# Decoder layer with a masked self-attention, a cross-attention and experts: end of a head, context halves and next loads moved

## What is computed

```python
x = layernorm(x + self_attention(x))            # causal, rope, 32 heads of 16
x = layernorm(x + cross_attention(x, context))  # 32 query heads of 128, 8 key/value heads, 1601 keys
x = layernorm(x + x @ base_W.T + lora(x))       # 28 experts of rank 8, top 2 by a gate
```

## Time and profile before

| | us |
|---|---|
| median of 3 runs | 2866.11 |
| lowest and highest | 2860.11 and 2867.98 |
| the profiled execution | 2861.03 |
| its span, first to last instruction | 2859.2 |

### The profile page before, as it was taken

One profiled execution on the slowest core, in us unless ns is written; L12 is line 12 of the kernel. 1 busy time (PEld: TensorE's weight loads), 2 busy tenths in 40 slices (PEclk: granted clock), 3 DMA queues, 4 the chain that ended last, 5 costly groups with the idle time before them and its releaser, 6 DMA issues. The chain is left out here.

```text
span 2859.2 us, 60441 instructions
## 1 busy us (share of the span) xinstructions
PE 2682.2 (94%) x20528; PEld 2488.0 (87%) x20528; DVE 2081.0 (73%) x4144; ACT 1943.2 (68%) x4158; POOL 1651.6 (58%) x1674
## 2 busy tenths in 40 slices
PE   7889999999889999999988999999988999999997
PEld 5789999898669999999867999999976899999995
DVE  4488787878548878787855878787775587878785
ACT  4476676667547777677664767777766576777674
POOL 3389898957216656565712656665551365656563
PEclk9999999999999999999999999999999999999998
DMA  6356464612411212121331112122142121213111
GB/s 212 129 176 226 166 225 163 210 53 80 174 45 39 97 53 97 48 102 45 119 120 52 67 68 74 67 71 79 55 158 80 51 82 53 97 45 104 45 53 59
DMA packets 89999, 281.69 MB, mean 99 GB/s; under 512 B 9056, under 2 KB 9184, under 8 KB 86624
## 3 DMA queue, kind: packets, MB, share of 16 engines
q1 hardware_dynamic: 89696, 277.82, 28.1%
HBM read 233.75 MB, written 44.04 MB: 97 GB/s over the span
## 5 line engine op out<-in xcount | busy, mean ns | idle before, releaser
L564 POOL TENSOR_TENSOR kept_s<-kept_s,mrow 128x512 f32<-128x512 f32 (+1 forms) x896 | 1065.6, 1220 | 574.1 <-ACT mrow L800 574.1
L1127 DVE TENSOR_TENSOR pl<-sp,ph 128x512 fp32r<-128x512 f32 (+1 forms) x896 | 576.2, 643 | 60.2 <-ACT sp L815 59.2
L810 ACT ACTIVATE ph<-kept_s 128x512 fp32r<-128x512 f32 (+1 forms) x896 | 534.0, 596 | 47.0 <-POOL kept_s L564 41.8
L815 ACT ACTIVATE sp<-kept_s 128x512 f32<-128x512 f32 (+1 forms) x896 | 506.3, 565 | 5.1 <-DVE sua L1135 5.0
L1201 PE MATMUL dn<-ph,vh 128*128 128x256 f32 (+1 forms) x1664 | 490.4, 295 | 2.3 <-DVE pl L1127 1.3
L1201 PE MATMUL dn<-ph,vl 128*128 128x256 f32 (+1 forms) x1664 | 472.9, 284 | 0.0
L1201 PE MATMUL dn<-pl,vh 128*128 128x256 f32 (+1 forms) x1664 | 471.8, 284 | 0.0
L1135 DVE TENSOR_TENSOR sua<-sp,sua 128x512 f32<-128x512 f32 (+1 forms) x640 | 399.6, 624 | 0.0
L792 ACT ACTIVATE kept_s<-bank 128x512 f32<-128x512 f32 x384 | 228.4, 595 | 226.1 <-PE bank L1201 224.5
L792 ACT ACTIVATE kept_s<-sp 128x512 f32<-128x512 f32 x384 | 228.5, 595 | 182.8 <-PE sp L1201 178.8
L1201 PEld LDWEIGHTS dn<-ph,vh 128*128 128x128 f32 (+1 forms) x1664 | 318.0, 191 | 10.4 <-DVE pl L1127 3.2
(11 more groups left out here) (161 smaller groups left out, 6622.7 us busy)
## 6 DMA issues: line engine op xcount, KB each, us to landing
wqx<-wq SPq DMA_DIRECT2D x128, 512.0 KB, 3.4
wox<-wo SPq DMA_DIRECT2D x64, 1024.0 KB, 4.9
wk<-wk SPq DMA_DIRECT2D x32, 512.0 KB, 3.3
wvx<-wv SPq DMA_DIRECT2D x16, 1024.0 KB, 6.9
craw<-in_ctx_t SPq DMA_DIRECT2D x16, 800.5 KB, 4.5
wqk<-in_ws SPq DMA_DIRECT2D x16, 513.0 KB, 5.5
raw<-in_wq_in SPq DMA_DIRECT2D x32, 256.0 KB, 4.0
wq<-hib SPq DMA_DIRECT2D x32, 256.0 KB, 2.0
```

Source lines behind the costliest of these rows:

```text
L564: nc.gpsimd.tensor_tensor(kept_s[:, n % 2, i:z, :], kept_s[:, n % 2, i:z, :], mrow[:, n % 2, :].unsqueeze(1).broadcast_to([P, z - i, S]), ...
L810: nc.scalar.activation(ph[:, k % PH, 0:cols], src, ACT.Exp, scale=XSCALE).then_inc(ph_ok, 1)
L815: nc.scalar.activation(pbank[k % 2][:, 0:cols], src, ACT.Exp, scale=XSCALE).then_inc(pr_ok, 1)
L1127: nc.vector.tensor_tensor(pl[:, k % PH, 0:cols], src, ph[:, k % PH, 0:cols], ALU.subtract).then_inc(pl_ok, 1)
```

## The change

Three things are moved; no arithmetic is added or left out.

The end of a head: VectorE takes the reciprocals in slot 7 in place of 6 and normalizes in slot 8 in place of 7, there at the head of the slot; TensorE spreads the reciprocals behind the jobs and the weighing of slot 7, no longer ahead of them. The context: GpSimd writes the high part too, each piece ahead of its low part, as soon as the quarter has landed; ScalarE's copies fall away. The border: x and the first weights are issued behind the last scores of the batch, ahead of SyncE's waits for the last Q and O jobs; the projection of Q is cut in two halves of two chunks, in slots 223 and 224.

```diff
--- before.py
+++ after.py
@@ -73,7 +73,7 @@
 
 
 SCORE, SHIFT, EXP, LOW, VALUE = -13, -4, -3, -2, 0
-MAX_TURN, MAX_COL, MAX_ROW, SUM_FOLD, SUM_COL, SUM_ROW, HEAD_SUM, HEAD_END = -6, -5, -4, 5, 6, 7, 7, 9
+MAX_TURN, MAX_COL, MAX_ROW, SUM_FOLD, SUM_COL, SUM_ROW, HEAD_SUM, HEAD_DIV, HEAD_END = -6, -5, -4, 5, 6, 7, 7, 8, 9
 SLOTS = range(SCORE, NSL * (NHB - 1) + HEAD_END + 1)
 
 
@@ -498,12 +498,13 @@
                             load_k(b * NP + (c + 1) // 2, (c + 1) % 2)
                         elif c + 1 == XKV:
                             load_k(b * NP + NP, 0)
+                    if b + 1 < nb and g == NSL * NHB + SCORE:
+                        sp.wait_ge(sc_mm, (b + 1) * NHB * NSL)
+                        sp.dma_start(xt[:, :, :], x_t[b + 1]).then_inc(xt_ld, 16)
+                        first_weights()
                     for j in JOBS[g]:
                         used(j)
                 if b + 1 < nb:
-                    sp.wait_ge(sc_mm, (b + 1) * NHB * NSL)
-                    sp.dma_start(xt[:, :, :], x_t[b + 1]).then_inc(xt_ld, 16)
-                    first_weights()
                     sp.wait_ge(rd_mm, (b + 1) * NHB)
                     load_context(b + 1, 0)
                 sp.wait_ge(pv_mm, (b + 1) * NHB * NSL)
@@ -542,6 +543,9 @@
             def ctx_low_part(b, m, k):
 
                 a, z = CTX_PIECES[k]
+                q = b * NM + m
+                pool.wait_ge(ctx_ld[q % CTX_SLOTS], 16 * (q // CTX_SLOTS + 1))
+                nc.gpsimd.tensor_copy(ctxh[:, m, a:z], craw[:, q % CTX_SLOTS, a:z]).then_inc(split_hi, 1)
                 pool.wait_ge(split_hi, b * CTX_N + m * len(CTX_PIECES) + k + 1)
                 nc.gpsimd.tensor_tensor(ctxl[:, m, a:z], craw[:, (b * NM + m) % CTX_SLOTS, a:z], ctxh[:, m, a:z],
                                         ALU.subtract).then_inc(ctx_ok, 1)
@@ -651,9 +655,6 @@
                     nc.scalar.activation(hgt[0:n, :, k, :], f_bank(b, "H")[0:n, k * S:(k + 1) * S].rearrange("p (t n) -> p t n", t=TB),
                                          ACT.Copy).then_inc(f_act, 1)
 
-            def high_part(hi, src):
-                nc.scalar.activation(hi, src, ACT.Copy).then_inc(split_hi, 1)
-
             for b in range(nb):
                 def take_qk(m):
 
@@ -705,14 +706,6 @@
                     if b * NQ + u >= PTQ:
                         act.wait_ge(s_pvq, (b * NQ + u - PTQ) // 2 + 1)
                     nc.scalar.activation(pt[:, n % (PTQ * QH4), :], s_turn[:, 0:3 * P], ACT.Copy).then_inc(s_ptc, 1)
-
-                def take_context(u, i):
-
-                    mc, k = divmod(2 * u + i, len(CTX_PIECES))
-                    q = b * NM + mc
-                    a, z = CTX_PIECES[k]
-                    act.wait_ge(ctx_ld[q % CTX_SLOTS], 16 * (q // CTX_SLOTS + 1))
-                    high_part(ctxh[:, mc, a:z], craw[:, q % CTX_SLOTS, a:z])
 
                 take_qk(0)
                 for u in range(NQ):
@@ -741,13 +734,11 @@
                     if b and u == 7:
                         deviation(b - 1, 2)
                     take_turned(u, 1)
-                    take_context(u, 0)
                     if m + 1 < NM:
                         if e == 0:
                             take_qk(m + 1)
                         else:
                             take_v(m + 1)
-                    take_context(u, 1)
                     if e == 0 and m:
                         take_heads(m - 1)
                     if b and u == 1:
@@ -1166,14 +1157,14 @@
                 for g in SLOTS:
                     for j in JOBS.get(g - 1, ()):
                         job_low(*j)
+                    for h in head_of(g, HEAD_DIV):
+                        normalize(h)
                     for h, s in slot_of(g, LOW):
                         low_and_sum(h, s)
                     for h in head_of(g, MAX_COL):
                         row_maxima(h)
-                    for h in head_of(g, SUM_COL):
+                    for h in head_of(g, SUM_ROW):
                         row_reciprocals(h)
-                    for h in head_of(g, HEAD_SUM):
-                        normalize(h)
                     for h, s in slot_of(g, SCORE):
                         if s:
                             maximum(h, s)
@@ -1255,7 +1246,7 @@
 
             def project_qk(t, kind, chunks):
 
-                if kind == 0:
+                if kind == 0 and chunks[0] == 0:
                     if t % NM == 0:
                         pe.wait_ge(xt_ld, at(t // NM, 16, 16))
                     pe.wait_ge(wqk_ld, at(t, 16, 16))
@@ -1533,18 +1524,21 @@
                         scores(h, s)
                     for h in head_of(g, MAX_ROW):
                         spread_maxima(h)
-                    for h in head_of(g, SUM_ROW):
-                        spread_reciprocals(h)
                     for j in JOBS[g]:
                         run_job(*j)
                     for h in head_of(g, SUM_COL):
                         sum_rows(h)
                     for h, s in slot_of(g, VALUE):
                         weigh(h, s)
+                    for h in head_of(g, SUM_ROW):
+                        spread_reciprocals(h)
                     for h in head_of(g, MAX_TURN):
                         turn_maxima(h)
-                    if b + 1 < nb and g in (NSL * NHB - 1, NSL * NHB):
-                        project_qk((b + 1) * NM, g - (NSL * NHB - 1), range(DC))
+                    if b + 1 < nb and g == NSL * NHB - 1:
+                        project_qk((b + 1) * NM, 0, (0, 1))
+                    if b + 1 < nb and g == NSL * NHB:
+                        project_qk((b + 1) * NM, 0, (2, 3))
+                        project_qk((b + 1) * NM, 1, range(DC))
                 run_job(*LAST_JOBS[0])
                 if b + 1 < nb:
                     swap_pairs((b + 1) * NM)
```

## The result

The kernel with the change takes 2838.1 us (median of 4 runs, 2833.3 to 2842.4) against 2865.0 us of the kernel before in the same session (2860.1 to 2868.0): ratio 0.9915, 95% interval 0.9898 to 0.9932, 26.8 us less. The prediction was 2853 us, 13 us less: the direction was right, the size half of what came. The traces can explain these 21.3 us; the other 5.5 of the 26.8 are how far each profiled execution lies from its median (2861.0 against 2865.0 before, 2839.7 against 2838.1 after).

A forecast was written before the change was run, and what follows sets the result against it. TensorE, busy 94% of the span, was taken as the bound, VectorE a close second in light intervals. 4.7 + 5.9 + 6.0 - 1.8 - 1.5 = 13.3 us less gave 2853 us, range 2838 to 2868.

The forecast's parts named there:

- The wait for the reciprocals: TensorE's 28.1 us before spreading: 4.7 us back in twelve V intervals, 5.9 in sixteen light ones (no K or V jobs).
- the waits would lie in light intervals alone: Sign in the profile after: waits before spreading reciprocals 8 to 12 us, only in light intervals, zero in V intervals.
- Failed step 1: Head's end: VectorE's waits for the sums over rows would go, without a price; reciprocals leaving its queue counted 0.08 us.
- Failed step 2: Clock in light intervals: six of sixteen pay 1.5 us; four were taken as won back, 6.0 us, bounds 0 and 9.
- Failed step 3: First batch's heads: folding of the maxima stays pinned by GpSimd, normalizing comes behind; 1.8 us lost, bounds 0 and 8.8.
- Failed step 4: Batch borders: GpSimd's context pieces collide with VectorE's rope products, halved projection gains 0.87 us; net 1.5 us lost over three.
- the context worth nothing to ScalarE: Context stage: ScalarE loses 16 copies a batch, 8.5 us, but does not set the pace; worth nothing.
- the earlier DMAs worth nothing: Border: five DMAs for x and first weights go ahead of SyncE's waits for the last O jobs; gain nothing.
- no wait moved in full to the maxima: Rival, chance 0.30: VectorE is the bound, TensorE's waits move to the maxima; only 1.4 us less, 2865 us.
- the waits come back in full: Rival: all of TensorE's waits for reciprocals return, 42 us less, 2824 us; chance 0.14 with the ground up to it.

The follow-up runs named there:

- e5: Kernel before plus spreading behind slot 7's weighing and normalizing in slot 8, but reciprocals still in slot 6: 2835.8 us, ratio 0.9913 to the kernel before.
- e9: e6 with normalizing ahead of the low part of Q in VectorE's slot 8: 2832.9 us, ratio 0.9892 to the kernel before.
- e2: Kernel before with only the context's casts moved from ScalarE to GpSimd: 2867.3 us, ratio 1.0024.
- e3: Kernel before with only the border part (Q projection halved, x and first weights issued earlier): 2862.8 us, ratio 1.0006.
- e7: Kernel before with only the normalizing moved, from slot 7 to the head of slot 8: 2857.6 us, ratio 0.9994.
- e8: e2, but from the second batch on GpSimd starts each context quarter only behind that quarter's masks: 2862.2 us, ratio 1.0008 to the kernel before.
- e1: Kernel before with only the new order of the head's end, context and border as before: 2833.7 us, ratio 0.9906.
- e4: Kernel before with the head's end and the border part, without the context part: 2834.7 us, ratio 0.9909.
- e6: e1 with the reciprocals in slot 7 ahead of low part and running sum, not behind: 2827.5 us, ratio 0.9887 to the kernel before.
- e10: e6 with ScalarE's copy of the head's weighted sum in slot 6, ahead of the exponentials: 2899.0 us, ratio 1.0125 to the kernel before.
- e11: e6 with the border part, without the context part: 2825.7 us, ratio 0.9871 to the kernel before.

## Why the prediction was half of what came

**The wait for the reciprocals: right in mechanism, its total right by luck.** The waits fell to 11.1 us (forecast 8 to 12) and the light interval to 13.04 us (forecast 13.0). But a light interval keeps 0.39 us of the wait where the prediction had 0.7, so the thirteen of them hold only 5.1 of the 11.1 us; the V intervals, where it had none, hold 2.2, and the last heads, h = 1 and single others the rest. Three of the sixteen intervals that the prediction multiplied with 0.37 us are h = 1 (13.9 us): two became 0.2 us longer and one 0.3 shorter. Three rows of a light interval, in the order TensorE, VectorE, TensorE, beside the earlier trace rows:

```profile
1609.22 0.39 PE L1192 MATMUL dn<-ph,vh 128*128 128x256 f32 x1
...
1610.37 0.16 DVE L1133 RECIPROCAL rs<-sp 128x2 f32<-128x2 f32 x1
...
1610.59 0.43 PE L1514 MATMUL sp<-cst,rs 128*128 128x128 f32 x2 [0.40 <-DVE rs L1133]
```

That the waits would lie in light intervals alone was wrong: a V interval has one too, beside the earlier trace rows, and is 0.30 us shorter where I had 0.39 (3.6 us for twelve, not 4.7):

```profile
1718.54 0.43 PE L1514 MATMUL sp<-cst,rs 128*128 128x128 f32 x2 [0.18 <-DVE rs L1133]
```

**Failed step 1: intervals with V jobs at h = 8, 16, 24 were costed at nothing.** The prediction summed TensorE's waits before the spreading and took the reciprocals out of VectorE's queue only as 0.08 us. VectorE's own wait (96.4 us in 71 waits) it names at the end as a thing that will go, without a price, and it never asked who stands behind it. It is worth 12 intervals of 0.5, 6.2 us. e5 gives the wait back and the 0.5 us with it, and so does e9 with another wait in its place.

**Failed step 2: "Between none and all six, I take four".** In the light intervals of the last three batches the upper bound, 9 us, was the value: none of these is below 1.00 after. In the last three batches the clock fell to a lower level in 28 of 60 light intervals of the five kernels where TensorE waits 1.1 us there (before 6, e2 5, e3 7, e7 4, e8 6, of 12 each), and in none of 96 of the eight where it waits 0.4 us or less before the spreading (after, e1, e4, e5, e6, e9, e10, e11). A drop costs 1.5 us, as the earlier trace rows had it. Two limits belong to this count. In e10 a light interval waits for 0.8 us in all, at other places, and none of its twelve fell. And in the first batch, where h = 3, 11 and 19 hold other waits of 1.7 to 3.7 us, the clock fell in 28 of 39 cases, in the kernels with the new order as in those without. So the clock was won back in these intervals; over the whole execution it was not (0.986 before and after), and how much of the 9 us reached the end is not settled.

**Failed step 3: the first batch, wrong in sign.** The prediction had 1.8 us lost, because the folding of the maxima would stay pinned by GpSimd. It came free of it. The folding in the first batch's heads, before and after (busy us, mean ns):

```profile
L1109 DVE TENSOR_TENSOR mxa<-mxa 128x256 f32<-128x256 f32 x31 | 31.3, 1009 | 1.1
```

```profile
L1100 DVE TENSOR_TENSOR mxa<-mxa 128x256 f32<-128x256 f32 x31 | 18.0, 581 | 1.1
```

Without the normalizing ahead of it, it stands at another place beside GpSimd's work; e7, with that move alone, has the same mean within 1%, so this move is the cause, and TensorE's wait for the folding falls with it (in e7 from 11.8 us to 2.2, as in the kernel after, though 6.2 us of waits for the normalizing come beside it in e7). The first batch's heads took 4.8 us less in the kernel after and 3.5 less in e7, but 1.4 more in e1, whose order there is that of the kernel after. The clock makes that difference: in these heads it stood at its lower level, 1.2 GHz, for 17 us before, 19 after and 32 in e1. With 0.44 us taken off for each of these us, an estimate from the light intervals with and without a drop, the heads took 562 us before, 558 in e7, and 556 to 557 in the seven kernels with the new order other than e10.

**Failed step 4: the borders, too cheap by 3 us (4.6 lost, 1.5 forecast).** The collision was there; VectorE and GpSimd at the last border of the kernel after, where the earlier trace rows show TensorE's side of before:

```profile
2113.70 0.53 POOL L548 CAST ctxh<-craw 128x400 fp32r<-128x400 f32 x1
2113.81 0.70 DVE L977 TENSOR_TENSOR qr<-t 128x256 f32<-128x256 f32 x1
...
2114.32 1.08 POOL L550 TENSOR_TENSOR ctxl<-craw,ctxh 128x400 fp32r<-128x400 f32 x1
2114.43 1.24 DVE L980 TENSOR_TENSOR kr<-t 128x256 f32<-128x256 f32 x1
2115.35 0.71 POOL L548 CAST ctxh<-craw 128x400 fp32r<-128x400 f32 x1
2115.60 1.71 DVE L989 TENSOR_SCALAR qm<-qr,cst 128x256 f32<-128x256 f32 x2
```

qr and kr take 1.3, 1.8 and 1.9 us together (forecast over 1.5 at each) and the masks, which I had left out, another 1.7 to 1.8 in place of 0.68. The cast holds VectorE up too, which the prediction found no row for: qr takes 0.70 us in place of 0.41 beside it. From projection to first score the kernel after takes 11.7, 9.7 and 9.9 us (the first with a drop of the clock), e4, which lacks only the context, 8.5 in all three: the collision costs 1.2 and 1.4 us where the clock held, near the forecast of 1.1. It is kr (0.83 us more), qr (0.1 and 0.3) and the first of the two masks (0.25) that TensorE waits for; the second mask is off the path. The 0.9 us of the halved projection are there too (9.4 to 8.5 in e3 and e4).

These stretches lose 3.1 of the 4.6 us. The other 1.5 lie before them, between the last turning and the projection, and are the clock's. At full clock the new order of the last head costs 0.1 us there: 17.3 us (e5's third border, e11's second and third) against 17.2 before. But the stretch takes 18.3 to 18.6 us where the granted clock in it is 0.91, with the new order (two borders of e1, the last of the kernel after) and with the old (the first border of before and of e3). The prediction had no term for the clock at the borders. Whether the new order makes the drop there more likely is not settled: the clock was at 0.91 or lower in 16 of 24 such stretches with the new order and in 3 of 15 without it, but where it was not it often fell just before or behind.

Nor did e3's 0.9 us a border reach the end. The self-attention stages of the last three batches took 92.9 to 95.8 us in all kernels, 94.6 or more in 8 of 12 cases with the border part (the kernel after, e3, e4, e11) and in 10 of 27 without it; all of these long ones have a drop of the clock in them. Whether the border's order does that, or chance, is not settled.

**Right:** the context worth nothing to ScalarE and a price at the border; the earlier DMAs worth nothing (e3, which holds them together with the halved projection, is no faster); no wait moved in full to the maxima. Of the rivals, "the waits come back in full" is nearest by time, 2824 us, but not by mechanism: light intervals did not get below 13.0, not even in e6, where the wait is gone; only e9's did, and gave it back. The Trainium skill (SBUF — State Buffer, Who interferes with whom) was right against this part. It says that VectorE's tensor_scalar, too, can take the port pair that VectorE shares with GpSimd, when its operands allow it. The trace agrees: beside GpSimd's casts and subtractions the masks took 1.71 us in place of 0.68. In which of its modes VectorE ran them, no run here shows.

## What to carry to other kernels

When an instruction is moved out of a queue, list the waits of every engine that held it, not only those of the busiest: what stood behind it there is freed too, and that may be what the busiest engine waits for in another stretch. A wait of about a microsecond on TensorE can cost more than itself when the clock falls behind it. Count in how many equal stretches it does, and look for stretches with a shorter wait: here the twelve V intervals of the kernel before, with a wait of 0.51 us each, had no drop, a hint of more than four. Then compare the clock of the whole span, before and after, since a drop that is gone in one stretch can stand in another. When two runs of the same order differ, set their time at the lower clock beside the difference before looking for a cause. And judge a local gain by the interval and the one behind it: e9 took 0.4 us from one and gave it to the next.

## What the runs showed that I had not expected

One wait of TensorE goes with the drops of the clock closely, in twelve equal intervals of thirteen kernels: with one wait of 1.1 us in an interval of 13.4 us the granted clock fell in 28 of 60 cases, with 0.4 us or less in its place in 0 of 96. It says nothing of intervals with other waits, as the first batch shows.

An instruction of VectorE with one tensor in SBUF and a column of scalars (the masks, 0.34 us each alone) is held up by GpSimd as those with two tensors are: 1.71 us for two beside a cast of 0.71 and a subtraction of 1.03 us. GpSimd's cast is held up as well, 0.71 us in place of 0.53.
